# Value copies ahead of the next input's load, weights folded at the last statistics tile, bias table by one selection matrix, attention set-up reordered

## The reference, cut to what matters

```python
# block 1: windows of 7 x 7 tokens; layernorm, a linear scan over the 49 tokens, layernorm, MLP
xB = xw @ Bm ; h_t = xB_t + h_(t-1) @ A ; y = h @ Cm
out = y + gelu(layernorm(y) @ W1 + b1) @ W2 + b2
x = x + block1(groupnorm(x))
# block 2: windows of 7 x 7 tokens on the image rolled by (-3, -3); 12 heads of 16 channels
attn = q @ k.T * 16**-0.5 + bias[head, n, m] + mask(window)
bias = rpb_table[rel_idx]          # rpb_table: 169 x 12, rel_idx from row and column distance
out = softmax(attn) @ v @ proj.T + proj_b
x = x + block2(groupnorm(x))
```

## Time and profile before

| | us |
|---|---|
| median of 3 runs | 4611.31 (4606.82 to 4611.5) |
| profiled execution | 4597.89 |
| its span | 4596.1 |
| statistics part | 0 to 151 |
| block 1 | 151 to 2440.9 |
| set-up of block 2, to the first transpose | 2440.9 to 2501.6 |
| units of block 2 | 2501.6 to the end |

### The profile page before, as it was taken

One profiled execution on the slowest core, in us unless ns is written; L12 is line 12 of the kernel. 1 busy time (PEld: TensorE's weight loads), 2 busy tenths in 40 slices (PEclk: granted clock), 3 DMA queues, 4 the chain that ended last, 5 costly groups with the idle time before them and its releaser, 6 DMA issues. The chain is left out here.

```text
span 4596.1 us, 142253 instructions
## 1 busy us (share of the span) xinstructions
PE 4316.2 (94%) x52232; PEld 3688.3 (80%) x52232; DVE 3933.2 (86%) x8105; ACT 2476.2 (54%) x4852; POOL 2584.1 (56%) x2092
## 2 busy tenths in 40 slices
PE   0599999999999999999995999999999999999998
PEld 0488888888888888888885888888888888888887
DVE  6698888888888888888872888888888888888888
ACT  0244444444444444444441666777776766776676
POOL 1155555555555555555542666666666666666666
PEclk9999999999999999999996999999999999999999
DMA  8011111111111111111111222222222222222222
GB/s 354 17 39 39 39 39 39 39 39 39 40 41 39 39 39 39 39 39 39 39 34 46 71 76 74 75 74 74 74 76 75 75 75 75 74 74 74 74 74 69
DMA packets 389849, 286.06 MB, mean 62 GB/s; under 512 B 147147, under 2 KB 388091, under 8 KB 388603
## 3 DMA queue, kind: packets, MB, share of 16 engines
q1 hardware_dynamic: 387060, 283.20, 21.2%
q10 hardware_dynamic: 2736, 2.14, 0.1%
HBM read 120.39 MB, written 87.31 MB: 45 GB/s over the span
## 5 line engine op out<-in xcount | busy, mean ns | idle before, releaser
L892 POOL TENSOR_TENSOR L<-L,mx 128x588 f32<-128x588 f32 x512 | 600.3, 1172 | 644.0 <-DVE mx L1118 643.9
L603 PE MATMUL ps_o<-w,g_hi 128*128 128x384 f32 x2352 | 711.1, 365 | 5.9 <-DVE g_lo L543 4.1
L415 ACT ACTIVATE gF<-ps_g,b1f 128x512 f32<-128x512 f32 x588 | 404.7, 688 | 392.9 <-PE ps_g L634 390.8
L886 POOL TENSOR_TENSOR E<-E,ri 128x588 f32<-128x588 f32 x512 | 600.0, 1172 | 0.8 <-DVE ri L1124 0.8
L1180 PE MATMUL ps_s<-Kp,Q 32*64 32x98 f32 x12288 | 494.5, 259 | 59.9 <-DMA Kp<-K 58.8
L603 PE MATMUL ps_o<-w,g_lo 128*128 128x192 f32 x2352 | 535.0, 255 | 0.0
L442 POOL TENSOR_TENSOR res<-xt,b2b 128x768 f32<-128x768 f32 x98 | 181.1, 1848 | 591.2 <-DVE x L491 591.2
L401 ACT ACTIVATE h_hi<-ps_h,hbias 128x512 fp32r<-128x512 f32 x196 | 123.1, 679 | 703.7 <-PE ps_h L618 703.7
L1114 DVE SCALAR_TENSOR_TENSOR L<-ps_s,bias 128x588 f32<-128x588 f32 x512 | 394.6, 771 | 92.2 <-PE ps_s L1180 76.5
L603 PEld LDWEIGHTS ps_o<-w,g_hi 128*128 128x128 f32 x2352 | 429.9, 189 | 26.8 <-issue 24.8
L999 ACT ACTIVATE o_hi<-ps_v,vb 128x98 fp32r<-128x98 f32 (+1 forms) x1024 | 289.1, 334 | 300.5 <-PE ps_v L1293 293.3
(11 more groups left out here) (222 smaller groups left out, 12495.5 us busy)
## 6 DMA issues: line engine op xcount, KB each, us to landing
xs<-in_x SPq DMA_DIRECT2D x8, 4704.0 KB, 22.2
xt<-in_x SPq DMA_DIRECT2D x98, 384.0 KB, 3.4
x_cells<-x SPq DMA_DIRECT2D x784, 48.0 KB
xb<-x_cells SPq DMA_DIRECT2D x128, 294.0 KB
Vx<-V SPq DMA_DIRECT2D x512, 73.5 KB
out<-yo SPq DMA_DIRECT2D x128, 294.0 KB
Kp<-K SPq DMA_DIRECT2D x256, 98.0 KB, 2.0
Kp<-K SPq DMA_DIRECT2D x256, 49.0 KB, 1.9
```

The lines of the kernel that those rows point to most:

```text
L415: act.activation(gF[f % 4][:, :], ps_g[:, f % 2, :], ACT.Gelu, bias=b1f[:, f:f + 1]).then_inc(s_gelu, 1)
L603: last = pe.matmul(dst, g[:, f, P * k:P * (k + 1)], w, start=(f == 0 and i == 0), stop=(f == FT - 1 and i == 1))
L886: pool.tensor_tensor(e, e, ri[p][:, :].unsqueeze(2).to_broadcast([P, HEADS, T]), ALU.mult)\
L892: pool.tensor_tensor(l, l, mx[p][:, :].unsqueeze(2).to_broadcast([P, HEADS, T]), ALU.subtract).then_inc(s_sub, 1)
```

## The change

Five things are done.

1. In the statistics part, the folding of the weights stands ahead of the last tile (k = 7) instead of tile 4.
2. The last step's second half of 7 store DMAs is issued by ACT's queue instead of SP's.
3. The bias table: `hot0`, `hot1`, `tab0`, `tab1` and the 49 pairs of small matmuls go. SP loads from the reversed 169-entry table, with overlapping strides, a table `tab` of 85 partitions x 49 x 12 in four DMAs; one selection matrix `query_row` (85 x 128) times it gives the bias of all queries for both window slots in two matmuls (504 and 84 columns). They stand first in PE's stream of the set-up.
4. The set-up is reordered: zeroing of buffers and the copies of the bias table stand on DVE between the steps of the statistics chain, the first input load is issued ahead of the wait for `s_par`, which stays in front of the parameters' load.
5. In the units, SP issues the four Vx copies ahead of the load for unit u+2.

```diff
@@ statistics, DVE
-                        if k == NT // 2:
+                        if k == NT - 1:
                             dve.wait_ge(s_w, 16 * WEIGHT_LOADS)
@@ block 1, SP, last step
-                        for q in range(2):
+                        for q in range(1 if isinstance(n, int) and n == STEPS else 2):
+                            store(sp, d, u, q)
@@ block 1, ACT, behind its last step
                 slots(act, slot)
+                act.wait_ge(s_x1, STEPS)
+                store(act, (STEPS - 1) % CHUNKS, (STEPS - 1) // CHUNKS, 1)
@@ set-up, SP
-                for dst, src in ((hot0[:, :, :], onehot[0:P]), (hot1[:, :, :], onehot[P:RPB]),
-                                 (groups[:, :], group_of), (tab0[:, :], rpb[0:P]), (tab1[:, :], rpb[P:RPB]), (mask[:, :, :], shift_mask)):
+                for high in ((SHIFT, WS), (0, SHIFT)):
+                    for wide in ((SHIFT, WS), (0, SHIFT)):
+                        ny, nx = high[1] - high[0], wide[1] - wide[0]
+                        first = SPAN * ((high[0] - SHIFT) % WS) + (wide[0] - SHIFT) % WS
+                        rows = bass.AP(rpb.tensor, rpb.offset + HEADS * first,
+                                       [[HEADS, REACH], [HEADS * SPAN, ny], [1, nx * HEADS]])
+                        sp.dma_start(tab[:, :, :].rearrange("p (i j) h -> p i (j h)", i=WS)
+                                     [:, high[0]:high[1], HEADS * wide[0]:HEADS * wide[1]], rows).then_inc(s_l, 16)
+                for dst, src in ((query_row[:, :], query_of), (groups[:, :], group_of), (mask[:, :, :], shift_mask)):
@@
-                sp.wait_ge(s_par, 1)
@@
                     sp.dma_start(xb[c][0:T2, :, :], src).then_inc(s_xb[c], 16)
+                    if isinstance(u, int) and u == 0:
+                        sp.wait_ge(s_par, 1)
@@ units, SP
-                    if is_unit(u + 2):
-                        upto(sp, s_rs, u + 1)
-                        upto(sp, s_vb, u + 1)
-                        load(i + 1, c)
                     if is_unit(u):
...
                                   .then_inc(s_vx[c], 16)
+                    if is_unit(u + 2):
+                        upto(sp, s_rs, u + 1)
+                        upto(sp, s_vb, u + 1)
+                        load(i + 1, c)
@@ set-up, DVE
                 link(last)
+                dve.memset(Q[1][:, :, :, :], 0.0)
+                link(dve.memset(params[:, :, :], 0.0))
                 dve.wait_ge(s_m2, 1)
...
+                dve.memset(Kp[1][:, :, :, :, :], 0.0)
+                dve.memset(Vx[0][:, :, :], 0.0)
+                dve.wait_ge(s_b2, 1)
+                for b in range(2):
+                    m0, m1 = MB * b, min(MB * (b + 1), T)
+                    last = dve.tensor_copy(base[:, :, m0:m1],
+                                           ps_b[:, b, 0:(m1 - m0) * HEADS].rearrange("p (m h) -> p h m", h=HEADS))
+                link(last)
                 dve.wait_ge(s_p2, 1)
@@ set-up, PE
+                pe.wait_ge(s_l, 16 * 7)
+                for b in range(2):
+                    m0, m1 = MB * b, min(MB * (b + 1), T)
+                    last = pe.matmul(ps_b[:, b, 0:(m1 - m0) * HEADS], query_row[:, :],
+                                     tab[:, m0:m1, :].rearrange("r m h -> r (m h)"), start=True, stop=True)
+                last.then_inc(s_b2, 1)
                 pe.wait_ge(s_v2, 1)
...
-                for m in range(T):
-                    dst = ps_b[0:T, m // MB, (m % MB) * HEADS:(m % MB + 1) * HEADS]
-                    pe.matmul(dst, hot0[:, m, :], tab0[:, :], start=True, stop=False)
-                    last = pe.matmul(dst, hot1[:, m, :], tab1[:, :], start=False, stop=True)
-                last.then_inc(s_b2, 1)
```

More of the change, by code:

```diff
@@ L340, in there, with store @@
                 return not isinstance(n, int) or 0 <= n < STEPS
+            def store(engine, d, u, q):
+                i = u // WS
+                a, b = (WS + SHIFT - 1 - i) // WS, (WS + SHIFT - 1 - u % WS) // WS
+                imgs = slice(2 * TPC * d + q, 2 * TPC * (d + 1), 2)
+                base = q * WINS
+                rows, cols = bass.ds(1 - a, CELLS), bass.ds(1 - b, CELLS)
+                row, col = bass.ds(CELLS + 1 - a, 1), bass.ds(CELLS + 1 - b, 1)
+                parts = [(x1[d][base:base + WINS, k, :],
+                          x1_cells[rows, imgs.start + 2 * k, cols, bass.ds(u, 1), :]
+                          .rearrange("r w t c -> r w (t c)")) for k in range(TPC)]
+                parts += [(x1[d][base:base + CELLS, :, :],
+                           x1_cells[row, imgs, cols, bass.ds(u, 1), :]
+                           .rearrange("r k w t c -> (r w) k (t c)")),
+                          (x1[d][base:base + WINS:CELLS, :, :],
+                           x1_cells[rows, imgs, col, bass.ds(u, 1), :]
+                           .rearrange("r k w t c -> (r w) k (t c)")),
+                          (x1[d][base:base + 1, :, :],
+                           x1_cells[row, imgs, col, bass.ds(u, 1), :]
+                           .rearrange("r k w t c -> (r w) k (t c)"))]
+                for src, dst in parts:
+                    engine.dma_start(dst, src).then_inc(s_st[d], 16)
             block = ctx.enter_context(nc.Block())
@@ L670, in build @@
             NG = NT * GROUPS
[L671 to L673 removed]
+            SPAN = 2 * WS - 1
+            REACH = (WS - 1) * (SPAN + 1) + 1
+            query_row, tab = sb("query_row", [REACH, P]), sb("tab", [REACH, T, HEADS])
             mask = sb("mask", [P, 4, T])
@@ L1053, in _ @@
                 last.then_inc(s_par, 1)
-                link(dve.memset(base[:, :, :], 0.0))
-                dve.memset(Q[1][:, :, :, :], 0.0)
-                dve.memset(Kp[1][:, :, :, :, :], 0.0)
-                for b in range(2):
-                    last = dve.memset(Vx[b][:, :, :], 0.0)
-                last.then_inc(s_i3, 1)
-                dve.wait_ge(s_b2, 1)
-                for w in range(2):
-                    for b in range(2):
-                        m0, m1 = MB * b, min(MB * (b + 1), T)
-                        last = dve.tensor_copy(base[SLOT * w:SLOT * w + T, :, m0:m1],
-                                               ps_b[0:T, b, 0:(m1 - m0) * HEADS].rearrange("p (m h) -> p h m", h=HEADS))
-                link(last)
                 for r in range(2):
@@ L1336, in shape_constants @@
     xi = WS * tok[:, 1] + tok[:, 3] - SHIFT
-    rel = (yi[:, None] - yi[None, :] + WS - 1) * (2 * WS - 1) + xi[:, None] - xi[None, :] + WS - 1
-    onehot = np.zeros(((2 * WS - 1) ** 2, T, T), f)
-    onehot[rel.T, np.arange(T)[:, None], np.arange(T)[None, :]] = 1
+    span = 2 * WS - 1
+    reach = (WS - 1) * (span + 1) + 1
+    query_of = np.zeros((reach, P), f)
+    for w in range(2):
+        query_of[reach - 1 - (span * yi + xi), SLOT * w + np.arange(T)] = 1
     mask = np.zeros((P, 2, 2, T), f)
@@ L1351, in shape_constants @@
     return {"image_mean": image_mean, "group_of": group_of, "identity": np.eye(P, dtype=f),
-            "onehot": onehot, "shift_mask": mask.reshape(P, 4, T)}
+            "query_of": query_of, "shift_mask": mask.reshape(P, 4, T)}
 def kernel(**inputs):
@@ L1380 @@
     arrays["proj_b"] = plain("L1_conv_proj_b")
-    arrays["rpb"] = np.ascontiguousarray(plain("L1_conv_rpb_table")[:, [2 * g + e for g in PAIR_AT for e in range(2)]])
+    arrays["rpb"] = np.ascontiguousarray(plain("L1_conv_rpb_table")[::-1, [2 * g + e for g in PAIR_AT for e in range(2)]])
     arrays.update(shape_constants())
```

32 lines of the change are left out of this document (4 added, 28 removed).

## The result

The changed kernel takes 4493.86 us (median of 4 runs, 4493.03 to 4495.77) against 4609.07 for the kernel before beside it; ratio 0.9753, 95% interval 0.9739 to 0.9766. Measured a second time, beside other runs of the kernel before, it took 4494.78 us (5 runs, 4491.63 to 4497.89), ratio 0.9762 (0.9749 to 0.9776). Its profiled execution took 4493.39 us, span 4491.6, against 4597.89 before.

A forecast was written before the change was run, and what follows sets the result against it. Units were held PE-bound but for the Kp wait, statistics bound by DVE and its waits, block 2's set-up by a serial chain. Gains 26.4 + 4.4 + 29.0 + 5 + 55 = 119.8 off 4611.3 gave 4491.5 us, range 4474 to 4527.

The forecast's parts named there:

- tiles 0 to 6 run without a stop: Statistics: tiles 4 to 6 land in time by 1.2 us, so DVE reaches tile 6's end at 96.8 us.
- all bytes decide when the weights are in: Statistics: 40.7 MB at 430 GB/s are in at about 97 us; weights taken at 97.5.
- last tile to 110.8, against 137.2: Statistics: fold done at 99.1 us, last tile ends at 110.8 instead of 137.2; gain 26.4 us.
- The halving: Block 1's last store: 14 issues of 8.88 us become 7 on each of two queues, 4.44 us; gain 4.4.
- The chain from landing to parameters: Set-up of block 2: bias matmuls, averaging, DVE steps, power, spreading, shifts and parameters sum to 18.1 us.
- the landing of the small loads: Set-up of block 2: all small loads there at t = 10.5 us (8 to 18), table at 27 GB/s.
- The estimate of 7.2 us: Set-up's table load: 238 runs on each of five engines at Vx's 30 ns a run.
- half of the clock's 4 us: First units: a bit over half the second unit's 4 us excess returns, within a 5 us gain; clock fall open.
- the whole 0.45 goes: Steady units: Kp lands with 1.5 us of slack, ending PE's 0.45 us wait per unit; gain 55 us.
- Next in line is PE itself: Steady units: with the wait for Kp gone, PE's own work sets the time, a unit of 15.7 us.
- The rival named VectorE: Units: another PE wait, on DVE or ACT, takes Kp's place; half the 55 us back, 4519 us; chance 0.16.
- Its own bounds: Whole kernel: the parts' bounds summed, with 45 to 57 us for the units, reach from 4482 to 4523 us.

The follow-up runs named there:

- u3: Changed kernel with the second half of block 1's last stores back on SyncE's queue, none on ScalarE's: 4493.34 us, one run.
- u1: Changed kernel with SP loading the input of unit u+2 ahead of the Vx copies again: 4539.13 us, ratio to before 0.9855.
- e3: Changed kernel with TensorE's two-unit loop cut behind the projections of the third step, same instructions and order: 4471.37 us, ratio to before 0.9709.
- e2: Changed kernel with SP's order in a unit made load, Kp copies, then Vx copies: 5259.0 us, one run.
- u4: Changed kernel keeping only new bias table and reordered set-up; fold, last stores and unit load order undone: 4571.5 us, ratio to before 0.9925.

## Why the prediction was right, and where its terms were off

The forecast of 4491.5 us lies 2.4 us from the median, and the mechanism of each part but the first units is the one foreseen. The closeness is in part luck. In the profile's own terms the forecast was 4478, and the profiled run took 4493.4: 15.3 us less gain than summed. The 13.4 us by which the median of before lay above its profile, carried over to the changed kernel, made up for it; the changed kernel's profile and median agree within 0.5 us.

- **Statistics, 26.4 forecast, 22.1 measured.** The step that tiles 0 to 6 run without a stop, and that all bytes decide when the weights are in, held; they came at 99.9 instead of 97.5 us (2.4). The term before it is off too: 40.7 MB at 430 GB/s from 1 us on end at 95.6, not at about 97. The step "last tile to 110.8, against 137.2" counted the chain behind it as before; L208 grew by 1.7 us beside GpSimd.
- **Last store, 4.4 and 3.4.** The halving is right, but an issue on ScalarE's queue took 0.79 us against 0.65 on SyncE's, and ScalarE's seven are last: 5.52 us where 4.44 were counted; the 1.6 us behind the last issue stayed. Issue time is what was gained, as the rule of the Trainium skill cited there (DMA: Bandwidth & Descriptors, on issuing engines) has it; u3 shows the same release 3.4 us later with all on one queue.
- **Set-up, 29.0 and 33.8.** The chain from landing to parameters was forecast at 18.1 us and took 18.8 (2421.72 to 2440.55, the end of L1074). L1058's 1.07 us, where a step and hand-over had 0.3, makes the difference. The mis-sized term is the landing of the small loads, 10.5 against 5.2. It was taken from 27 GB/s, the tail of the one-hot load. While the table came, 72 GB/s flowed and 0.39 of the DMA engines' time was busy, about six of sixteen:

```profile
2417.60:2419.20 1.60, 0.00 (x0) 0.00 (x0) 1.60 (x2) 0.00 (x0) 0.00 (x0) 0.50 0.39 72
```

The Trainium skill (DMA: Bandwidth & Descriptors, why a DMA increments its semaphore by 16) deals 85 partitions to five engines. The trace is near it and far from sixteen, but five would be 0.31. The estimate of 7.2 us made from it failed on the other factor: the 30 ns for a run was the Vx copies' pace, which is that of their issues, 0.85 us each. Here 200 KB at 72 GB/s are 2.8 us, an estimate of 12 ns a run if five engines share 1190. Nor is the table all of the 5.2 us: the seven issues take 3.5 (2416.55 to 2420.02), and TensorE's wait ends with the last of them, the mask, 1.7 later. How much a faster table alone would give is not shown.
- **First units, 5 and 4.9.** The number is luck. The sum was 2.4 us for Kp and half of the clock's 4 us, and said that it is open whether the clock falls. It falls in some executions: 39.4 us at 0.87 and 43.9 at 0.80, the same kernel. At equal clock (0.80) 0.4 of the 5 us are left. Its bounds, 0 to 8, hold both.
- **The steady units, 55 and 41.4.** The step "the whole 0.45 goes" is right for the wait, and u1 shows that the queue order is its cause. "Next in line is PE itself" was right, but the engine's own instruction stream was not free: the loop's end, 0.31 us in every second unit, had been under the wait for Kp. The loop's end accounts for 18.8 us from 2500 to 4440, and only 13.6 are missing. The 5 us between come from two things: TensorE's busy time in a unit is a little shorter too, 15.69 us against 15.73, which no run explains, and the table's row holds some four units more than the window of the 55 us. e3 takes the loop's end away and gains 22.5 us. The rival named VectorE as what may lie under the pause; it was TensorE's own queue, and half as large.
- **The range.** Its own bounds were added up with 45 us for the units, where the section on the units has 25. With 25 they reach to 4543, above the 4527 given; the measured time is in either.

## What to carry to other kernels

When a wait goes, look for what ended inside it, the engine's own loop end included; a loop can be cut where a long instruction is still running. On an in-order queue put the copies that are ready first, ahead of a wait for something later, and check the same move in the wrong direction: here it cost seventeen times the gain (765 us, one run, against 45). Before a gain of a few us is put down to a part, profile the same kernel twice: here one stretch of 40 us differed by 4.5 us between two executions, with the clock. Take the price of a DMA from a row of the same limit (issue or landing), not from the nearest pace.

## What the runs showed of the hardware

- Four units in a loop pass instead of two took the instruction loads from 0.56 to 6.31 MB, TensorE stopped for 4.6 us in a pass, and the granted clock was 0.89, 0.50 for some 18 us behind the long stop.
- With a stop of 2.4 us in each unit the clock was 0.78 over 2560 us, and 0.50 for some 6 us behind the stop shown (e2); with stops of 0.45 us it was 1.00 or 0.99 (u4).
- The same kernel got 0.87 and 0.80 in its first units in two executions, 39.4 and 43.9 us.
- A two-input VectorE instruction beside a long two-input one on GpSimd took 2.34 us instead of 0.61 and ended 0.47 us after it. The Trainium skill (VectorE: DVE Perf Modes, on two Vector instructions with no wait between them) calls the second read interface of such an instruction shared with GpSimd; that fits this instruction. It does not explain L1058, which took 1.07 us beside a clearing, which reads nothing.
- The end of a loop pass of two units cost TensorE 0.31 us behind short matmuls (changed kernel) and showed no idle time behind long ones (e3).
